# ScalarE writes the places of a pair's rows behind the copy of the transposed q instead of ahead of the copy of the transposed heads

## The reference

```python
h = tok(x)                              # sum of position, nesting and segment embeddings, times W
h = h + attn(layernorm(h))              # 8 heads of 64, chunks of 128 tokens
h = h + ffn(layernorm(h))               # 8 experts of 512, the 2 best per token

# attn, per chunk of 128 tokens and head; q, k, v are 64 wide
q1, k1 = exp(q @ proj.T - max), exp(k @ proj.T - max)
D      = q1 @ sum(k1) ;  context = k1.T @ v
out    = (q1 @ context) / (D + 1e-4) ;  result = out @ w_out.T + b_out

# ffn: softmax over 8 gates, the two best divided by (their sum + 0.01);
# y = sum of weight * (relu(x @ W1[e] + b1[e]) @ W2[e] + b2[e]) over the two experts
```

## Time and profile before

| | us |
|---|---|
| timed runs (3) | 371.57, 367.45, 370.96; median 370.96 |
| profiled execution, whole | 368.57 |
| its span in the profile | 366.8 |
| TensorE matmuls busy | 334.7 (91%) |
| VectorE busy | 303.0 (83%) |
| ScalarE busy | 244.8 (67%) |
| GpSimd busy | 195.1 (53%) |
| TensorE clock granted, mean | 0.949 |

### The profile page before, as it was taken

One profiled execution on the slowest core, in us unless ns is written; L12 is line 12 of the kernel. 1 busy time (PEld: TensorE's weight loads), 2 busy tenths in 40 slices (PEclk: granted clock), 3 DMA queues, 4 the chain that ended last, 5 costly groups with the idle time before them and its releaser, 6 DMA issues.

```text
span 366.8 us, 11920 instructions
## 1 busy us (share of the span) xinstructions
PE 334.7 (91%) x3273; PEld 296.6 (81%) x3273; DVE 303.0 (83%) x1190; ACT 244.8 (67%) x722; POOL 195.1 (53%) x345
## 2 busy tenths in 40 slices
PE   7948999999999988999997979999999999999983
PEld 3616788787787777777876879999999999999983
DVE  7585799999997888988897448889997777878986
ACT  1634777878776887778786247876776777776640
POOL 6010231766664765656765437787876545555430
PEclk9965899999999999999998569999999999999998
DMA  6084740000010000101000202223333222226767
GB/s 162 27 238 128 215 174 2 25 26 26 28 34 32 27 27 16 32 32 32 21 23 26 81 8 68 84 79 94 97 119 108 89 70 77 67 79 191 223 208 229
DMA packets 33131, 30.47 MB, mean 83 GB/s; under 512 B 4701, under 2 KB 27320, under 8 KB 33080
## 3 DMA queue, kind: packets, MB, share of 16 engines
q1 hardware_dynamic: 25848, 18.81, 17.8%
q0 software_dynamic: 4224, 9.18, 7.1%
q10 hardware_dynamic: 3008, 1.89, 1.9%
HBM read 16.42 MB, written 13.44 MB: 81 GB/s over the span
## 4 chain that ended last, share of the span: by engine, by line
PE 68%; DVE 17%; issue 8%; ACT 4%; DMA 1%; DVEq 1%; SPq 1%; ACTq 0%
PE ps_oy L1815 9%; PE ps_v L1815 9%; PE ps_out L1805 9%; PE ps_q L1805 7%; PE ps_oy L1726 6%; PE ps_out L1711 5%; PE ps_qT L1698 4%; PE ps_qT L1797 2%; PE ps_k L1805 2%; PE ps_oy L1719 2%; ACT oT L873 2%; DVE k_prime L1090 2%; DVE q_prime L1090 2%; PE ps_k L1661 2%; DVE stats L1067 1%
## 5 line engine op out<-in xcount | busy, mean ns | idle before, releaser
L776 POOL DMA_INDIRECT y_dram<-heads_out,place x68 | 69.4, 1020 | 44.2 <-ACT heads_out L966 33.4
L754 POOL DMA_INDIRECT slots_dram<-rows,row_id x64 | 63.6, 993 | 20.2 <-issue 19.4
L957 ACT ACTIVATE k_prime<-ps_out,b_T 128x128 f32<-128x128 f32 x105 | 31.1, 365 | 19.9 <-PE ps_out L1805 19.1
L728 POOL TENSOR_TENSOR rstd<-moments,ln_eps 128x4 f32<-128x4 f32 (+1 forms) x19 | 3.7, 195 | 74.9 <-DVE moments L1073 74.8
L957 ACT ACTIVATE k_prime<-ps_q,b_T 128x128 f32<-128x128 f32 x108 | 31.9, 366 | 17.2 <-PE ps_q L1805 17.0
L1815 PE MATMUL ps_oy<-w_tile,k_prime 128*128 128x128 f32 x288 | 38.3, 276 | 1.1 <-issue 1.1
L1726 PE MATMUL ps_oy<-out_w,oT 128*128 128x128 f32 x256 | 37.9, 294 | 0.0
L1815 PE MATMUL ps_v<-w_tile,k_prime 128*128 128x128 f32 x280 | 37.1, 276 | 0.4 <-issue 0.3
L1711 PE MATMUL ps_out<-context,qT 64*128 64x65 f32 x512 | 37.2, 287 | 0.0
L1805 PE MATMUL ps_out<-sT,w_tile 128*128 128x128 f32 x280 | 37.0, 275 | 0.0
L1815 PEld LDWEIGHTS ps_oy<-w_tile,k_prime 128*128 128x128 f32 x288 | 35.0, 192 | 1.6 <-issue 1.6
(11 more groups left out here) (280 smaller groups left out, 856.3 us busy)
## 6 DMA issues: line engine op xcount, KB each, us to landing
qkv_rows<-slots_dram SPq DMA_DIRECT2D x71, 72.0 KB
y_sum<-y_dram SPq DMA_DIRECT2D x14, 256.0 KB, 3.4
w_all<-in_L_ffn_W SPq DMA_DIRECT2D x1, 2048.0 KB, 13.8
w_all<-in_L_ffn_W SPq DMA_DIRECT2D x8, 256.0 KB, 4.4
out<-h SPq DMA_DIRECT2D x6, 256.0 KB, 3.7
y_dram<-heads_out,place POOLq DMA_INDIRECT x68, 2.3
y_dram<-y_sum SPq DMA_DIRECT2D x2, 512.0 KB, 4.5
slots_dram<-rows,row_id POOLq DMA_INDIRECT x64, 2.3
```

What stands on the lines that cost most here:

```text
L754: nc.gpsimd.indirect_dma_start(slots_dram[:, :], bass.IndirectOffsetOnAxis(row_id[:, place_of(p, a), j, k:k + 1], 0), rows[:, place_of(p, ...
L776: nc.gpsimd.indirect_dma_start(y_dram[:, :], bass.IndirectOffsetOnAxis(place[:, a, :], 0), y[:, a, :], None).then_inc(s_placed[a], 16)
L957: last = nc.scalar.activation(hT[:, a % 2, c, :], ps_up[a % 2][0][:, c * P:c * P + P], ACT.Relu, bias=b1_T[:, bass.ds(experts[0] * FC + c, ...
```

## The change

In ScalarE's `sequence`, the call of `row_places` goes from behind `exps_of` (ahead of `oT_copy`) to behind `qT_copy`. Nothing else differs.

```diff
                 if live(p - 3):
                     exps_of(p - 3)
-                    row_places(p - 3, 1 - a)
                 if live(t - 1, TILES):
                     oT_copy(t - 1, 1)
                 if live(t + 1, TILES):
                     k_exp(t + 1, a, 1)
                     qT_copy(t + 1, 1)
+                if live(p - 3):
+                    row_places(p - 3, 1 - a)
 
                 if live(p - 2):
                     wait(act, s_slots[a], 16 * 2 * TOP * (half - 1))
```

## The result

The changed kernel takes 356.31 us, the median of four runs (355.45 to 357.27), against 370.18 (367.45 to 371.57) for the kernel before. The ratio is 0.9635, with an interval from 0.9569 to 0.9701: 13.9 us faster by the medians, where I had forecast 8.6. The profiled execution took 355.64 us, of which 353.9 are its span; before, 368.57 and 366.8. In the experiments the times of a kernel are medians and the ratios compare means, and a run over 1.5% above its kernel's fastest on the same chip is left out of both.

A forecast was written before the change was run, and what follows sets the result against it. TensorE and VectorE were nearly full, delayed by ScalarE's wait for the mask ahead of oT. Terms of 4.9 (loop), 2.8 (pairs 3 to 6), 0.2 and 0.7 us sum to 8.6; 370.96 - 8.6 = 362.4 us, range 357.5 to 366.8.

The forecast's parts named there:

- The mechanism: ScalarE waits for the mask ahead of the places (16.2 us); oT behind holds TensorE's y product (9.3 us).
- ScalarE's times: Pair 12 after the change: oT at about 163.2 us, k_exp 164.3, qT 164.9, places 165.4, normalisation 165.8.
- TensorE offers 0.82 us, VectorE can take 0.86, and the pair shrinks by the smaller.: Loop pairs 8 to 13: each shrinks 0.82 us, from 11.22 to 10.4, 4.9 us in all.
- VectorE's cap: VectorE's waits in a loop pair, 0.17 us for y plus 0.69 for k, limit the gain to 0.86 us.
- about 9 us by waits alone: Upper bound of the whole gain, as a loop pair can gain no more than VectorE's 0.86 us.
- Pairs 3 to 6, 0.70 us each: Written-out pairs: gaps of 0.72 us, VectorE's wait for k 0.70 us; four times 0.70 gives 2.8 us.
- a wait that I had costed at nothing: ScalarE's normalisation waiting for GpSimd's scatters: costed at nothing, as they are issued a pair earlier.
- Pair 7 nothing, pair 14 0.16 us: Pair 7 has no gap ahead of the y product; in pair 14 only VectorE's 0.16 us wait for y goes.
- The new pause of up to 0.56 us in pair 14: TensorE running ahead of VectorE pauses up to 0.56 us; the clock might fall there, in a slower rival of chance 0.03.
- Pair 15, 0.72 us: TensorE's 1.75 us wait for the mask stays, its 0.72 us wait for oT goes; half-clock stretch as long as now.
- the rival to which I gave 0.12: Clock stays up or returns sooner in the 17 us half-clock stretch: 4.3 us more off, 358.1 us; chance 0.12.
- The base: The 8.6 us sum was taken off the median of three timed runs, 370.96 us, not the profiled execution's 368.57.

The follow-up runs named there:

- the filled pair: Kernel before and changed kernel, each with seven idle matmuls on zeros ahead of the rank products of pair 15: 367.54 and 356.30 us.
- the second experiment: New order in the calls p = 3 to 14, old order in pair 15, against the kernel before: 359.4 us, ratio 0.9756.
- the third: New order in the six pairs of the hardware loop alone, against the kernel before: 362.72 us, ratio 0.986.
- the first experiment: New order in pair 15 alone, old order in all others, against the kernel before: 367.67 us, ratio 0.9959.
- the tenth: Changed kernel with six added activations (1.2 us) that wait for nothing, ahead of oT in pairs 3 to 15: 364.18 us, ratio 0.9897 to the kernel before.

## Why the prediction was right in kind and short in size

By its own steps:

- *The mechanism: ScalarE stands for the mask, and oT behind it holds TensorE.* Right, and shown by more than the result. The same amount of work without a wait at the same place costs a loop pair nothing (10.07 to 10.23 us with or without it); the wait with its work costs 1.03 us. With the places between oT and k_exp half of the gain is left.
- *ScalarE's times.* Right. Against the start of the last gate exponential, k_exp was to begin 1.3 us later and the places 2.4 us later; they did at 1.31 and 2.42. The wait for the shifted k was forecast at 0.5 to 1 us a pair, and is 0.64.
- *"TensorE offers 0.82 us, VectorE can take 0.86, and the pair shrinks by the smaller."* This is the step that failed for the loop: 1.03 us a pair, 6.2 us instead of 4.9. The 0.83 us of the earlier trace rows is counted from the end of the last rank product. In the rows an instruction that doesn't wait begins before the one ahead of it has ended: the y product of the changed kernel at 147.33, ahead of the end of the last rank product at 147.31 + 0.17 = 147.48. From the start of the first rank product to the start of the y product there were 165.51 - 164.40 = 1.11 us before, and there are 147.33 - 147.19 = 0.14 now: 0.97 us, and not 0.83. VectorE's cap was short for the same reason: from chosen_at to h it was 166.84 - 166.50 = 0.34 us and is 149.40 - 149.30 = 0.10, which is 0.24 where the row says 0.17, and from row_id to the head maximum there were 167.92 - 167.05 = 0.87 us and are now 149.72 - 149.60 = 0.12, which is 0.75 where the row says 0.69. The two make 0.99. The other kernels say the same with other numbers: 0.50 us seen cost 0.55, 0.18 seen cost 0.40. The last 0.04 to 0.06 us of the 1.03 stay open. So the top of the range, "about 9 us by waits alone", was no bound either. The two rows of before that this needs beside the earlier trace rows:

```profile
164.40 0.18 PE L1752 MATMUL ps_ln<-mask,before 128*128 128x8 bf16 x1
...
166.50 0.18 DVE L1160 TENSOR_TENSOR chosen_at<-chosen,row_at 128x32 f32<-128x32 f32 x1
```

- *Pairs 3 to 6, 0.70 us each.* 0.91, 0.32, 0.91 and 0.95: 3.09 us instead of 2.8. Three are larger for the reason above. Pair 4 is smaller because of a wait that I had costed at nothing, and which did come up once:

```profile
76.48 0.88 ACT L884 ACTIVATE rows<-h,shift,rstd 128x128 f32<-128x128 f32 x2 [0.70 <-DMA slots_dram<-rows,row_id]
```

  It is no accident of this execution: all eight traces with the new order in pair 4 and the gap closed have this wait there, of 0.32 to 0.99 us, and pair 4 takes between 10.0 and 10.5 us where pair 3 takes 9.8.

- *Pair 7 nothing, pair 14 0.16 us.* Right: 0.08 and 0.19. The new pause of up to 0.56 us in pair 14 came too (0.59 us ahead of the context product, for qT), and the granted clock stayed at full behind it.
- *Pair 15, 0.72 us, "what follows is TensorE's own chain", and a half-clock stretch as long as now.* This is the step that failed most: 3.61 us. Some 0.97 of it is the gap, counted as above, and about 2.6 is the clock, which was at half for twice 3.4 us instead of 17, and whose change the sum put at nothing. That is the rival to which I gave 0.12 and a price of 4.3 us. It did not come instead of the forecast but with it, and partly.
- *The base.* The sum by these terms is 13.17 - 0.25 = 12.9 us instead of 8.6, which is 4.3 of the 6.1 us between the forecast of 362.4 and the 356.31 measured. The rest, under 2 us, comes from setting it on the median: the profiled execution before, from which the rows are, lay 2.4 us under the median of 370.96, and the one after only 0.7 us under its own.

How much of the 13.9 us is the clock, and how much the order? The stretches show the clock at full or at half and at nothing between, so the time at half clock of each run can be estimated as (1 - mean clock) x 2 x span: for the profiled execution before 0.051 x 2 x 366.8 = 37.4 us, for the one after 0.039 x 2 x 353.9 = 27.6. All 37 runs of the kernel before beside these experiments range from 27.7 to 43.0 us, and their times from 365.7 to 372.2. Three of them had 27.7, with spans of 364.0, 364.2 and 364.9 us; three runs of the changed kernel had 27.6 or 27.7, with 353.7, 353.9 and 355.2. So the order by itself is worth some 10.1 us at an equal clock (the pairs of the table without the clock: 6.2 + 3.1 + 0.1 + 0.2 + 1.0 = 10.6, less 0.25 for the start), and the filled pair gave 11.2, or some 10 with its own difference of the clock taken off. The other 3 to 4 us are less time at half clock. Not all of this time lies near pair 15: the half-clock stretch of the start, from 22 to 24 us on, is 17 us long in five of the fourteen traces of this record, with the first rank product at 64.3 to 64.7 us, and 20.5 us long in nine, with that product at 66.1 to 66.8. The traces of the kernel before and of the change both have the short one.

What the change does to the clock is shown only as a tendency, counted over a line of 36 us that I drew after I had seen the runs. Of the kernels that keep the gap in pair 15 with the pause ahead of it, 21 runs of 45 had more than 36 us at half clock (before 16 of 37, the second experiment 3 of 4, the third 2 of 4). Of those in which the gap is closed by the new order, 4 runs of 34 had (none of 10 of the first experiment, none of 4 each of the change itself, with two activations ahead and with the tiles later, one of 4 each where the places stand behind oT and behind the context copy, 2 of 4 with six activations). None of 24 had with the pause filled or with the order at the end changed. The third experiment, with the gap and a short stretch, and the tenth, with no gap and a long one, show that the gap neither forces the long stretch nor is needed for it. What decides in one execution stays open.

## What to carry to other kernels

Look for an instruction that waits on a slow producer and stands, in an engine's program, ahead of work whose input has long been there: what it costs is the waiting, not its own time, and putting it behind the ready work, up to and including what TensorE needs next, took nothing from any loop pair here. Size the gain by the distance from start to start of the instructions around the gap, less the same distance in a place where nothing waits, and not by the idle time that the row shows, which was a fifth too small in the loop here. Where TensorE's clock falls behind a pause, give a change of that fall a term of its own in the sum, and look whether another small pause in the next microseconds goes as well.

## What the runs showed of the hardware that was not expected

- The half clock of the kernel before outlasted work end to end. TensorE had no pause from 199.94 to about 209.4 us, then one of 0.44 us and one of 2.04, and stayed at half clock until 216.5, 17 us after the fall. In the changed kernel the same matmuls, 0.9 us closer behind the rank products, were back at full clock 3.4 us after the fall. Rows of the kernel before show its side.

```profile
201.00:202.00 1.00, 1.00 (x7) 0.78 (x6) 0.00 (x0) 0.74 (x2) 0.22 (x1) 0.50 0.00 0
...
209.00:210.00 1.00, 0.56 (x3) 0.43 (x4) 0.69 (x6) 0.00 (x0) 0.00 (x0) 0.50 0.00 0
```

- The Trainium skill, "TensorE: Matmul & The Clock Gate", section "What's actually happening", says that the check of the activity runs freely and isn't aligned with the kernel's work. The runs agree with it but can't show the reason: one and the same kernel had between 27.7 and 43.0 us at half clock, and its times, which spread over 6.5 us, rise with it by 0.24 to 0.34 us per microsecond (a straight line through the runs of each chip).
- Matmuls on zeros, read by nobody, can keep the clock up: seven in a pause of 1.75 us took the median time at half clock of the kernel before from 33.1 to 27.8 us, on the same chip.
